# Delta rule of a two-layer model: the four-step loops of TensorE, ScalarE, GpSimd and VectorE start at an earlier step

## The reference, cut to what matters

```python
attn = jnp.where(strict_lower, -(k_beta @ jnp.swapaxes(k, -1, -2)), 0.0)
for i in range(1, chunk):                 # chunk = 32: the inverse of a unit lower triangle
    ...
u = attn @ v
w = attn @ k_beta
def step(S, inp):                         # one chunk after the other, the state S goes on
    q_i, k_i, u_i, w_i = inp
    attn_i = jnp.where(lower_incl, q_i @ jnp.swapaxes(k_i, -1, -2), 0.0)
    u_adj = u_i - w_i @ S
    o_i = q_i @ S + attn_i @ u_adj
    S = S + jnp.swapaxes(k_i, -1, -2) @ u_adj
    return (S, o_i)
```

## Time and profile before

| | us |
|---|---|
| median of 3 runs | 1336.69 |
| lowest and highest | 1327.07, 1341.28 |
| profiled execution, its own time | 1338.71 |
| its span, first to last instruction | 1337.1 |

### The profile page before, as it was taken

One profiled execution on the slowest core, in us unless ns is written; L12 is line 12 of the kernel. 1 busy time (PEld: TensorE's weight loads), 2 busy tenths in 40 slices (PEclk: granted clock), 3 DMA queues, 4 the chain that ended last, 5 costly groups with the idle time before them and its releaser, 6 DMA issues. The chain is left out here.

```text
span 1337.1 us, 35808 instructions
## 1 busy us (share of the span) xinstructions
PE 1194.5 (89%) x12725; PEld 889.9 (67%) x12726; DVE 773.6 (58%) x1827; ACT 478.6 (36%) x1157; POOL 496.5 (37%) x711
## 2 busy tenths in 40 slices
PE   7999999989999999983889898268888999889998
PEld 5888888867777777751444454247777888746665
DVE  5778878845222222224888898456655567435554
ACT  1112111123222222221888788213333344323332
POOL 3433666622531111107677545323343444210000
PEclk9999999989999999995999998568898899869999
DMA  9999920012321111112265534743463344200001
GB/s 315 369 352 383 376 61 33 33 40 69 124 97 64 63 63 63 63 44 78 66 177 146 134 107 140 156 122 87 96 127 80 104 122 112 89 0 24 32 29 43
DMA packets 220106, 156.61 MB, mean 117 GB/s; under 512 B 111888, under 2 KB 201488, under 8 KB 219984
## 3 DMA queue, kind: packets, MB, share of 16 engines
q1 hardware_dynamic: 210672, 129.51, 32.9%
q0 software_dynamic: 9312, 25.44, 5.6%
HBM read 64.47 MB, written 90.44 MB: 116 GB/s over the span
## 5 line engine op out<-in xcount | busy, mean ns | idle before, releaser
L945 PE MATMUL ps_sc<-w,a_qeo 128*128 x568 | 181.5, 463 | 0.0
L945 PEld LDWEIGHTS ps_sc<-w,a_qeo 128*128 128x128 f32 x568 | 103.1, 192 | 45.7 <-issue 1.0
L753 DVE TENSOR_TENSOR a_stm<-a_vpad,ps_sc 128x352 f32<-128x352 f32 x71 | 37.0, 521 | 161.5 <-ACT a_vpad L517 157.3
L423 POOL DMA_DIRECT2D x_slots<-a_stm x66 | 36.5, 552 | 216.7 <-issue 216.7
L1476 DVE SCALAR_TENSOR_TENSOR d_cout<-d_cin,d_taps,d_cout 128x512 f32<-128x512 f32 x144 | 101.7, 744 | 18.2 <-ACT d_cout L1352 18.1
L1633 PE MATMUL d_pp<-d_xT,d_w_p 128*128 128x512 f32 x192 | 105.1, 679 | 6.2 <-ACT d_xT L1334 6.2
L913 PE MATMUL ps_kv<-w,a_stm 128*128 x426 | 103.7, 379 | 1.2 <-DVE a_stm L746 1.2
L913 PEld LDWEIGHTS ps_kv<-w,a_stm 128*128 128x128 f32 x426 | 80.9, 190 | 24.1 <-issue 2.4
L2080 PE MATMUL u_bank_g<-u_qkT 64*64 64x256 f32 x256 | 70.7, 453 | 26.0 <-DMA u_kve<-rec 23.3
L2443 PE MATMUL g_pp<-g_xT,g_w_g 128*128 128x512 f32 x192 | 90.6, 610 | 0.7 <-ACT g_xT L2295 0.7
L517 ACT ACTIVATE a_vpad<-ps_sc 128x352 f32<-128x352 f32 x71 | 33.0, 465 | 156.5 <-PE ps_sc L945 136.2
(11 more groups left out here) (281 smaller groups left out, 2760.0 us busy)
## 6 DMA issues: line engine op xcount, KB each, us to landing
x_slots<-a_zeros SPq DMA_DIRECT2D x32, 1024.0 KB, 10.7
rec<-d_kve SPq DMA_DIRECT2D x32, 384.0 KB, 3.0
u_kve<-rec SPq DMA_DIRECT2D x32, 384.0 KB, 3.9
a_qeo<-x_slots SPq DMA_DIRECT2D x71, 128.0 KB
x_slots<-a_stm POOLq DMA_DIRECT2D x66, 128.0 KB
rec<-d_act_out SPq DMA_DIRECT2D x32, 256.0 KB
u_qkT<-rec SPq DMA_DIRECT2D x32, 256.0 KB, 3.3
w<-in_w SPq DMA_DIRECT2D x4, 1408.0 KB, 14.6
```

Of the source, the lines that this page charges most:

```text
L945: mm = pe.matmul(ps, e_xT[:, q, k, :], w13[:, s, k, bass.ds(e_hidden, 1), :], start=(k == 0), stop=(k == KD - 1))
```

## The change

Four calls of `pipelined` change their last argument; SP's call is not touched. Without `singly`, `lo` is the multiple of four at or above `depth + 1` = 6, so 8. DVE is given `max(ROWS_AT) + 1`, and the keys of `ROWS_AT` go from 0 to 7 (line 1003), so that `singly` is 8 and `lo` is 8 there too, though the title of the change names step 12 for VectorE. On all four engines the loop then makes six turns, steps 8 to 31, in place of four turns, steps 16 to 31; the eight steps 8 to 15 are no longer written out.

```diff
# GpSimd, ScalarE and TensorE, each:
-            pipelined(pool, NT, DEPTH, step, unroll=4, singly=GROUP * PART[1] + 1)
+            pipelined(pool, NT, DEPTH, step, unroll=4)
# VectorE:
-            pipelined(dve, NT, DEPTH, step, unroll=4, singly=GROUP * PART[1] + 1)
+            pipelined(dve, NT, DEPTH, step, unroll=4, singly=max(ROWS_AT) + 1)
```

More of the change, by code:

```diff
@@ L1963, in step @@
                     z.then_inc(s_out, 1)
-            pipelined(act, NT, DEPTH, step, unroll=4, singly=GROUP * PART[1] + 1)
+            pipelined(act, NT, DEPTH, step, unroll=4)
         @block.vector
@@ L2194, in step @@
                     mm.then_inc(o_done, 1)
-            pipelined(pe, NT, DEPTH, step, unroll=4, singly=GROUP * PART[1] + 1)
+            pipelined(pe, NT, DEPTH, step, unroll=4)
 def gated_output(nc, kept, ident, loaded, x_res, out):
```

## The result

The changed kernel takes 1391.43 us (1389.06 to 1398.0, four runs); the kernel before, run beside it, 1337.95. The ratio is 1.044, 95% interval 1.040 to 1.048: 53 us slower where 16 us of gain were forecast. The profiled execution took 1389.44 us, 50.7 more than that of before.

The account below looks back on a forecast made before the run. PE was taken as the bound, stalled by late code on first passage; fewer first passages from a fixed 991.06 us start step 21 15.9 us earlier: 1338.7 - 15.9 = 1322.8, less 2.0 for the median, 1321 us; range 1312 to 1332.

Parts of the forecast that it names:

- What bounds the kernel: PE sets the pace; late code stalls it on first passage, so steps 16 to 19 cost 10.9 us more than later turns.
- Their code is there by then: Steps 12 to 15, as second turn, find their code present; stalls of 1.00 and 2.48 us fall away.
- The rival that said so: Loop no longer fits: body touches eight packets, nine needed with the one fetched behind; returns find code missing; chance 0.10.
- The rival's price: Loop no longer fitting: turns at 39.4 instead of 28.5 us, five times, 54.5 us against 15.9, giving 1375 us; chance 0.10.
- The gain that the forecast had in mind: Looping from step 8 starts step 21 15.9 us earlier, by saving first passages in steps 12 to 19.
- The sum up to step 21: From 991.06 + 0.3, the rest of step 13 (5.65 us) and seven steps (49.9 us) put step 21 at 1046.9.
- the stall in step 32: Behind the loop, a code stall of 2.98 us may fall away or come twice: 3 us either way, taken as nothing.
- SP's sends as the fixed point: Steps 9 to 13: SP's sends delay tile 12's load; PE's step 13 waits until 991.06, which does not move.
- That the title's step 12 for VectorE makes no difference: If DVE looped from step 12, the sum would be the same; steps 9 to 12 do not wait for DVE.
- Only the third turn gains: Rival: tiles 12 to 15 come too late, steps 12 to 15 stay at 36.0 us, total 1325.8; chance 0.18.
- Straight code costs nothing and branches cost: Rival: stalls are not from first passage; 1336.7 us, or 1349 if five returns each stall 2.5 us; chance 0.04.
- about 3 us: Upper bound for a later step 13: 1.05 us shows past the load's wait, or about 3 with clock; 0.3 taken.

Follow-up runs that it names:

- the run with four instructions: Changed kernel with eight more waits ahead of PE's step 0, which become four instructions and move its loop head onto a packet border: 1310.9 us against 1334.4, ratio 0.985.
- the run with PE alone at step 8: Changed kernel with eight waits (four instructions) ahead of PE's step 0, and ACT, POOL and DVE put back to looping from step 16: 1310.2 us against 1332.55, ratio 0.982.
- the run with 90: Kernel before, looping from step 16, with 180 waits ahead of PE's step 0 that become 90 instructions: 1333.59 us against 1334.4, ratio 1.000.
- the run with 126: Kernel before, looping from step 16, with 252 waits ahead of PE's step 0 that become 126 instructions: 1384.16 us, ratio 1.037.

## Why the prediction was wrong

*What bounds the kernel* was right: PE, its first passage through code, stalls of 0.4 to 3.0 us with the granted clock at 0.83 to 0.94 in their stretches (they stand one to three borders apart, not at "every third packet"). The run with four instructions shows both halves: 41.3 us at 0.88 in the first turn, 28.6 and 28.5 us at 1.00 in the next two.

*"Their code is there by then"*, said of steps 12 to 15, is the step that failed. The code was there at no return: 113 packets in place of 68 are nine more for each of five returns. The second turn took 43.0 us in place of 28.5, the four after it 41.9 to 45.7. The rival that said so, with its border four instructions behind the new loop head, had 0.10. I had counted the border right and then let "any padding at the loop's head" talk me out of it, for which there was no row; the stall at 987.25, one matmul into the body, shows that there is no padding. The rows did speak, though none showed a ninth packet: with the one that is fetched behind the body, before made eight packets, none of which came again, and the new body makes nine. That PE can hold eight and not nine no row of before showed, and that a packet behind the body is fetched at all was my supposition then. The runs showed both: with 90 instructions ahead of the kernel before, a body of eight packets brought none in its later turns, and the changed kernel brought nine between two returns for a body of eight.

*The rival's price* was too low: 1375 us for 1391. I took a turn at 39.4 us; it takes 43.3. The difference is the return. Going back, PE finds the first packet missing, gets four instructions from it and finds the next one missing: 18.4 us in ten waits, 3.7 a return. With 43.3 the sum is 5 x 14.8 - 15.9 = 58 us, where 53 were measured.

*The gain that the forecast had in mind* is there once the head is moved: from 1334.4 to 1310.9 us and from 1332.55 to 1310.2, 23.5 and 22.4 us, where 15.9 were forecast. The sum up to step 21 came out: it gives 1046.9 - 953.3 = 93.6 us from the end of step 8, and in the run with four instructions steps 9 and 21 start 93.2 us apart (columns of these rows: start, us, line):

```profile
944.19 0.68 PE L2094 MATMUL u_bank<-u_S,u_qkT 128*128 128x128 f32 x4
...
1037.39 0.68 PE L2094 MATMUL u_bank<-u_S,u_qkT 128*128 128x128 f32 x4
```

Most of the missing part is behind the loop: the stall in step 32, which I had left at nothing within 3 us either way, is gone. The starts of steps 32 and 33, before and then in the run with four instructions:

```profile
1141.31 0.68 PE L2092 MATMUL u_bank<-u_S,u_qkT 128*128 128x128 f32 x4
1153.74 1.17 PE L2092 MATMUL u_bank<-u_S,u_qkT 128*128 128x128 f32 x4
...
1115.83 0.68 PE L2094 MATMUL u_bank<-u_S,u_qkT 128*128 128x128 f32 x4
1122.83 0.68 PE L2094 MATMUL u_bank<-u_S,u_qkT 128*128 128x128 f32 x4
```

Step 32 takes 7.0 us in place of 12.4.

*SP's sends as the fixed point* did not set the pace in the runs that gained. Tile 9's and tile 12's loads, in the run with four instructions and then in the run with PE alone at step 8 (columns: start, us, line):

```profile
944.38 0.38 SPq L1849 DMA_DIRECT2D u_x<-t_mat  x1
...
976.39 0.39 SPq L1849 DMA_DIRECT2D u_x<-t_mat  x1
...
951.37 0.38 SPq L1849 DMA_DIRECT2D u_x<-t_mat  x1
...
981.65 0.39 SPq L1849 DMA_DIRECT2D u_x<-t_mat  x1
```

Tile 12's load starts 32.0 and 30.3 us after tile 9's, where it was 32.3 before: the point moves by 2 us from run to run. Neither run has a wait for that load in step 13; PE's own first passage took about as long. That the sum came out within 0.4 us is thus luck in part: the wait from which it starts did not occur.

*That the title's step 12 for VectorE makes no difference* can't be told from these runs, but all of DVE's change makes none that can be measured. *Only the third turn gains* was wrong: with the code held, steps 12 to 15 run at 28.6 us. *Straight code costs nothing and branches cost* was wrong too: the same run goes back five times without a stall, at 0.21 to 0.23 us a branch. The "about 3 us" that the prediction names for the end of step 8 does not come out of its terms (1.05 us, doubled, is 2.1); the sum did not use it.

PE goes back over seven packets without a stall in the runs with four instructions and with PE alone at step 8, and there the longer loop is 1.5 and 1.8% faster than the kernel with eight more steps unrolled (ratios 0.985 and 0.982).

What stays open: whether the oldest packet is replaced or the one used longest ago, which in a loop is the same; where between 9 and 45 instructions in the last packet the loss begins, and whether the count of instructions or the time since the entry decides it.

## What to carry to other kernels

Count the packets of code that a loop touches, not its instructions, and add the one that is fetched behind it: here eight were held and nine were not, and one instruction on the wrong side of a border cost 74 us, where all that the loop saved was 22 to 24. Borders can be read from a trace of before, since straight code stalled at some of them (eight stalls of 0.4 to 2.7 us between 940 and 1062 us), and a few idle instructions ahead of the loop, here four, move its head. When a count from rows says that a limit is reached exactly, give that case the weight of the count, and don't set it aside for a mercy that no row shows.

## What the runs showed of the hardware

- PE's code comes in packets of 16,384 bytes (every one of the 113 on queue 8 in the changed kernel's trace) with 256 instructions each: the stalls at 995.02 and 1011.51 us of the kernel before stand 768 instructions apart, and from a count by 256 came the places of the stalls four instructions into the changed body (987.25 us) and nine instructions ahead of the branch in the run with 90 (1050.96 us). First passage in the kernel before, steps 8 to 19 and 32, stalls at borders one to three apart, for 0.4 to 3.0 us.
- Eight packets are held and nine are not: a body that touches eight and ends nine instructions into the last has no code packet in its later turns (81 in the whole run), one that ends 45 or 87 into it brings nine at each return (108 in the whole run).
- PE's branch back at the end of a turn takes 0.21 to 0.23 us when its target is held (the run with four instructions), and 3.3 to 3.9 us when it is not (the changed kernel).
- One instruction made the difference between 1310.9 and 1385.05 us, with the same program otherwise.
- The packet behind the body is ordered somewhere between 9 instructions (the run with 90: no code packet in the later turns) and 45 instructions (the run with 126: nine at each return) after PE has entered the last one, though no instruction of it is needed before the loop ends.
